# A 256-step recurrence inside a decoder kernel: its weights in four column tiles of 32, its input terms in two of 64 with a filler product behind them

## The reference, cut to what matters

```python
u  = einsum('bsd,nd->bsn', x, Wi) + bi
sp = einsum('bsd,nd->bsn', x, Ws) + bs

def step(state, inp):
    u_t, sp_t = inp
    state = tanh(state @ A.T + u_t @ B.T) + sp_t
    return state, state @ C.T

_, ys = scan(step, zeros, (u, sp))        # 256 steps, one after another
out = einsum('bsn,dn->bsd', ys, Wo) + bo
```

## Time and profile before

| | us |
|---|---|
| median of 3 runs | 1328.63 |
| profiled execution, its own time | 1330.58 |
| span of the profiled execution | 1328.9 |
| PE busy in the span | 1046.6 (79%) |
| ACT busy in the span | 672.7 (51%) |
| DVE busy in the span | 896.4 (67%) |
| recurrence, from the first step's product to step 255's | 1038.89 to 1208.92 |

### The profile page before, as it was taken

One profiled execution on the slowest core, in us unless ns is written; L12 is line 12 of the kernel. 1 busy time (PEld: TensorE's weight loads), 2 busy tenths in 40 slices (PEclk: granted clock), 3 DMA queues, 4 the chain that ended last, 5 costly groups with the idle time before them and its releaser, 6 DMA issues.

```text
span 1328.9 us, 18554 instructions
## 1 busy us (share of the span) xinstructions
PE 1046.6 (79%) x6579; PEld 679.0 (51%) x6579; DVE 896.4 (67%) x2076; ACT 672.7 (51%) x1863; POOL 644.2 (48%) x617
## 2 busy tenths in 40 slices
PE   5667978898788889888888978888854999998321
PEld 3354555465455546545554654555543665664321
DVE  3348776968787796878779687877976000444598
ACT  3746846764684686468468646844520123332000
POOL 1137656746765674676567467656841000111032
PEclk9769998999999999999999999999985679998655
DMA  6000000000000000000000000000000000000301
GB/s 167 1 4 9 1 1 12 1 1 5 8 1 1 13 1 1 5 9 1 1 13 1 1 1 1 1 1 1 1 17 0 0 1 2 7 8 5 32 16 32
DMA packets 56810, 12.76 MB, mean 10 GB/s; under 512 B 40318, under 2 KB 56462, under 8 KB 56590
## 3 DMA queue, kind: packets, MB, share of 16 engines
q1 hardware_dynamic: 56718, 11.58, 4.1%
HBM read 9.46 MB, written 2.12 MB: 9 GB/s over the span
## 4 chain that ended last, share of the span: by engine, by line
PE 40%; DVE 34%; ACT 10%; POOL 10%; issue 4%; DMA 1%; SPq 0%; POOLq 0%; DVEq 0%; ACTq 0%
PE bank_d L1672 5%; PE score_banks L1379 5%; PE score_banks L1731 4%; PE bank_a L1360 4%; DVE qm_s L1025 4%; DVE stats L887 3%; PE score_banks L1381 3%; DVE k_sin L1015 3%; PE score_banks L1380 3%; DVE kr_s L1019 3%; DVE prob L1079 3%; PE score_banks L1402 2%; PE out_bank L1624 2%; DVE o_rec L1071 2%; POOL psum L584 2%
## 5 line engine op out<-in xcount | busy, mean ns | idle before, releaser
L505 POOL TENSOR_TENSOR var_eps<-mv,epsilons 128x2 f32<-128x2 f32 (+2 forms) x64 | 12.7, 199 | 405.9 <-DVE mv L890 405.9
L765 ACT ACTIVATE prob<-score_banks 128x512 f32<-128x512 f32 x256 | 152.5, 596 | 104.3 <-PE score_banks L1381 101.8
L584 POOL TENSOR_TENSOR psum<-psum,prob 128x512 f32<-128x512 f32 x64 | 109.2, 1707 | 121.4 <-DVE prob L1079 120.9
L1379 PE MATMUL score_banks<-qm_s,kr_s 128*128 128x512 f32 x256 | 139.1, 543 | 29.9 <-DVE kr_s L1019 29.0
L1079 DVE TENSOR_SCALAR prob<-prob 128x1024 f32<-128x1024 f32 x128 | 111.1, 868 | 50.0 <-ACT prob L765 49.8
L1559 PE MATMUL out_bank<-prob,v 128*64 128x256 f32 x896 | 115.2, 389 | 2.4 <-DVE on L1072 2.3
L1025 DVE SCALAR_TENSOR_TENSOR qm_s<-q_raw,pair_mask,qm_s 128x256 fp32r<-128x256 f32 x128 | 80.7, 671 | 52.1 <-ACT qm_s L733 52.1
L582 POOL TENSOR_TENSOR psum<-prob 128x512 f32<-128x512 f32 x64 | 92.0, 1437 | 38.3 <-DVE prob L1079 38.3
L1380 PE MATMUL score_banks<-qm_s,kr_s 128*128 128x512 f32 x256 | 108.7, 425 | 0.0
L1381 PE MATMUL score_banks<-qm_s,kr_s 128*128 128x512 f32 x256 | 108.1, 422 | 0.0
L692 ACT ACTIVATE prob<-prob,neg_max 128x128 f32<-128x128 f32 (+1 forms) x256 | 106.2, 421 | 0.0
(11 more groups left out here) (336 smaller groups left out, 2627.0 us busy)
## 6 DMA issues: line engine op xcount, KB each, us to landing
cb<-in_ctx_dram SPq DMA_DIRECT2D x8, 256.0 KB, 2.8
bias_mask<-bias_scratch SPq DMA_DIRECT2D x1, 1536.0 KB, 7.3
xb<-in_x_dram SPq DMA_DIRECT2D x8, 128.0 KB, 2.1
prob<-in_L_xattn_Wkv_dram SPq DMA_DIRECT2D x1, 1024.0 KB, 6.6
att_scratch<-on SPq DMA_DIRECT2D x16, 64.0 KB, 3.1
prob<-att_scratch SPq DMA_DIRECT2D x2, 512.0 KB, 4.0
out_dram<-v SPq DMA_DIRECT2D x4, 256.0 KB, 2.3
prob<-in_L_xattn_Wq_dram SPq DMA_DIRECT2D x1, 512.0 KB, 7.4
```

What stands on the lines that cost most here:

```text
L584: link(g.tensor_tensor(psum[:, p % 2, :], psum[:, p % 2, :], pp[:, 2, :], ALU.add))
L765: s.activation(prob[:, p % 2, kb, :], sc[:, kb % 2, :], ACT.Exp, scale=DH ** -0.5).then_inc(exp_done, 1)
L1379: mm(out_ap, a_high, b_low, start=True, stop=False, **kw)
```

## The change

Three things are edited, all on PE. The product of each step is written in four column tiles of 32 output rows instead of two of 64. Each third of the input terms is written as two products of 64 output rows (columns 0 to 63 and 64 to 127 of the array) instead of one of 128. Behind each of these thirds a filler with 96 columns is added.

```diff
-KEEP = 192
-HALF_ROWS = P // 2
+KEEP, KEEP_Z = 192, 96
+HALF_ROWS, STEP_ROWS = P // 2, P // 4
...
-            def keep_clock():
-
-                mm(bank_d2[0:HALF_ROWS, 0:KEEP], ident[:, 0:HALF_ROWS], w_qkv_t[:, 0:KEEP], start=True, stop=True,
+            def keep_clock(columns=KEEP):
+
+                mm(bank_d2[0:HALF_ROWS, 0:columns], ident[:, 0:HALF_ROWS], w_qkv_t[:, 0:columns], start=True, stop=True,
                    skip_group_check=True)
...
             def z_third(part, third):
 
                 lo = Z_FIRST + P * part
-                bank = cf[:, lo:lo + P]
-                if third == 0:
-                    mm(bank, bwi_t, x3_t[:, lo:lo + P], start=(lo % 512 == 0), stop=False, skip_group_check=True)
...
+                for half in range(0, P, HALF_ROWS):
+                    of = slice(half, half + HALF_ROWS)
+                    bank = cf[of, lo:lo + P]
+                    if third == 0:
+                        mm(bank, bwi_t[:, of], x3_t[:, lo:lo + P], start=(lo % 512 == 0), stop=False,
+                           skip_group_check=True)
...
             def step(t):
                 pe.wait_ge(h_ready, t)
-                for lo in range(0, P, HALF_ROWS):
-                    last = mm(cf[lo:lo + HALF_ROWS, t * B:(t + 1) * B], a_t[:, lo:lo + HALF_ROWS],
+                for lo in range(0, P, STEP_ROWS):
+                    last = mm(cf[lo:lo + STEP_ROWS, t * B:(t + 1) * B], a_t[:, lo:lo + STEP_ROWS],
                               hid[:, (t - 1) * B:t * B], start=False, stop=True, skip_group_check=True)
                 last.then_inc(z_ready, 1)
...
                 if t <= 3 * Z_PARTS:
                     z_third(*divmod(t - 1, 3))
+                    keep_clock(KEEP_Z)
                 else:
                     keep_clock()
```

More of the change, by code:

```diff
@@ L1719, in z_third @@
                 lo = Z_FIRST + P * part
-                bank = cf[:, lo:lo + P]
-                if third == 0:
-                    mm(bank, bwi_t, x3_t[:, lo:lo + P], start=(lo % 512 == 0), stop=False, skip_group_check=True)
[L1723 to L1726, removed]
+                for half in range(0, P, HALF_ROWS):
[4 more added lines that the diff above has]
+                           skip_group_check=True)
+                    elif third == 1:
+                        mm(bank, aws_t[:, of], x3_t[:, lo - B:lo + P - B], start=False, stop=False,
+                           skip_group_check=True)
+                    else:
+                        mm(bank, c_rows[:, D + half:D + half + HALF_ROWS], one_row[:, 0:P], start=False, stop=True,
+                           skip_group_check=True)
             def step(t):
                 pe.wait_ge(h_ready, t)
-                for lo in range(0, P, HALF_ROWS):
-                    last = mm(cf[lo:lo + HALF_ROWS, t * B:(t + 1) * B], a_t[:, lo:lo + HALF_ROWS],
+                for lo in range(0, P, STEP_ROWS):
+                    last = mm(cf[lo:lo + STEP_ROWS, t * B:(t + 1) * B], a_t[:, lo:lo + STEP_ROWS],
                               hid[:, (t - 1) * B:t * B], start=False, stop=True, skip_group_check=True)
```

## The result

The changed kernel takes 1375.61 us (median of 4 runs, 1375.47 to 1377.65) against 1329.03 for the kernel before (4 runs, 1327.88 to 1329.70). The ratio is 1.0355, with a 95% interval from 1.0337 to 1.0373: slower by 3.5%. The forecast was 1332.4 in a range from 1325 to 1352, so it was wrong. It named the mechanism that did this, as a rival with a chance of 0.19, and priced it at 46 us if it struck in the first sixteen late steps, which its range left out.

What follows compares the result with a forecast made beforehand. The recurrence was taken as limited by PE and its drains at tile-shape changes, elsewhere by the chain of product and tanh. -7.8 + 6.0 + 5.6 = +3.8 us gave 1334.4, set to 1332.4 from the runs' median; range 1325 to 1352.

Steps and rivals of the forecast that it cites:

- The step's product in four tiles: Each step's product on PE: ends 0.04 us sooner, 0.25 us after its first load; chain-limited steps take 0.525, not 0.565.
- Filler steps at the full clock: Steps 37 to 127: PE drains at both width changes, 0.655 us a step, 59.6 us against 53.59, 6.0 us lost.
- Steps 1 to 36: Input-term steps: 0.705 us, every third 0.86, at the full clock; 27.2 us against 35.04, a gain of 7.8 us.
- Late steps at the full clock: The 128 late steps: eighty fillers cost 7.2 us, other intervals gain 1.6 us, in sum +5.6 us.
- The clock in the late steps: Rival: clock falls to half there and stays; 6 us if in the last sixteen, 46 in the first; chance 0.19.
- No drain between column tilings: Rival: 32 and 64 rows count as one mode, the chain limits every step, -22.7 us, 1306 us; chance 0.08.
- Tiles one behind the other: Rival: the two input-term tiles run one after the other in steps 1 to 36, +7.7 us, 1340; chance 0.04.
- The clock falling in steps 1 to 36: Rival: clock stays low or falls there, steps 37 to 127 stay at 1.1 us, some 100 us more; chance 0.02.

Runs made afterwards that it cites:

- e2: Changed kernel with step, input terms and fillers of the recurrence all in tiles of 32 rows; 1310.87 us, ratio 0.9857 to the kernel before.
- e1: Changed kernel with its step back in two tiles of 64 rows, the same width as input terms and filler; 1314.08 us, ratio 0.9882 to the kernel before.
- e3: Changed kernel with one filler more behind step 128, the first late step; 1332.20 us, ratio 1.0013 to the kernel before.
- e4: Changed kernel keeping only the four-tile step, input terms back in one product of 128 rows without filler; 1419.12 us, ratio 1.0673 to the kernel before.
- e6: Changed kernel with five fillers of 192 columns ahead of the recurrence, nothing inside it touched; 1431.94 us, ratio 1.0765 to the kernel before.
- e11: Changed kernel with ten fillers ahead of the recurrence; four executions took 1379.18, 1378.31, 1378.92 and 1337.07 us.
- e5: Changed kernel with the recurrence all in 32 rows and the constants' product over 128 input rows, zero-padded; 1307.57 us, ratio 0.9830 to the kernel before.
- e9: Changed kernel with five fillers ahead of the recurrence and the constants' product over 128 input rows; 1376.45 us, ratio 1.0351 to the kernel before.

## Why the prediction was wrong, point by point

*The step's product in four tiles: right on PE, half as large at ACT.* It ends 0.25 us after its first load, as forecast. But tanh starts 0.32 us after that load (1085.26 to 1085.58 in e2), not 0.30: it stands 0.07 us after the product's end, where the earlier trace rows have 0.05. So the gain where the chain limits is 0.02 us a step (0.545 against 0.565), and the forecast had 0.04 (0.525). e2 shows it alone.

*Filler steps at the full clock: right.* 0.648 against 0.655 forecast; +5.3 us against +6.0. The drain from 64 rows to 32, which the forecast took over from the rule and from the way in the other direction, is shown by the changed kernel's rows, and its absence between equal widths by e1 and e2. Where nothing drains a step of 32 rows takes 0.545, so the two drains cost 0.10 us a step.

*Steps 1 to 36: right.* 0.705 and 0.852 against 0.705 and 0.86, at the full clock; -7.9 us against -7.8. The tiles run side by side.

*Late steps at the full clock: right in size,* +5.4 in e3 against +5.6.

*The clock in the late steps: the step that failed.* The forecast summed the late steps as if the clock held, and gave its fall a chance of 0.19. It fell in all 4 executions, in the fifth late step, and the late steps took 129.31 us where the sum had 87.0 (81.40 + 5.6). The working saw the danger in the mean of a sixteen (240 to 270 columns a microsecond) and named as thinnest the stretch "around places 15 to 3". What it missed is that the first sixteen is thinner than the other seven: place 0 has no products there, because `early(b - 1, 16)` starts with the second batch. e3 puts one filler into that hole and 43 us are gone. It also gave the moment at which the hole comes no weight. Its argument against the fall was that the clock had never fallen there before and that the steps of the thin part get shorter. They did not in sum: the step with a filler in the hole got longer by what the others gained, and the hole takes 3.02 us before and after. That it had been harmless before was seen at the moments of the kernel before alone, and was weak ground for setting the fall at 0.19. The price was right: 46 us if in the first sixteen, 42.5 measured ((129.31 - 86.81) us in the late steps). So was the rest of that rival: in a loop with drains the clock doesn't come back (e4, e6).

*The rivals.* No drain between column tilings: refuted by the rows after. Tiles one behind the other: refuted. The clock falling in steps 1 to 36: not in the changed kernel, but in e6, which runs them 1.9 us later. The forecast gave it 0.02 and a price of some 100 us; e6 lies 99.7 us above e3, whose clock holds (1431.94 and 1332.20).

*What stays open.* Whether the kernel before would keep its clock in the hole at the changed kernel's moment; it kept it in every execution on record, but at its own moments. What exactly separates e11's one execution that kept its clock from its other three. And what the chip counts. The runs show that what PE runs in the hole counts (e3) and that a shift of the start counts (e6, e11), and no more. So the fall is shown as the failed step and the hole as its place, while the share that the drains have in it stays open.

## What to carry to other kernels

Count the width of a product's tile as part of its neighbours' cost: here a small product between fillers of another width gained 0.04 us on PE and paid two drains for it (0.648 us a step in place of 0.565), and the fix is to give all of them one width (e2, 1.4% faster than before), input rows too (e5, 1.7%). Where a chain of small products lives by fillers, look for the thinnest place of the order, at the ends of loops and in their first pass above all, not for the mean; a fall there lasts for the whole rest of the chain (42.5 us here), and one filler in the hole costs 0.10 us. A thin place that was harmless in one kernel need not be so after an edit elsewhere: run the kernel at a few shifted starts before trusting it, as e6 and e11 do. A loop that didn't lift the clock once it was down (1.06 us a step, e4 and e6) must be priced at both levels.

## What the runs showed of the hardware that was not expected

Moving an unchanged recurrence by five fillers moved the fall of the clock from its 132nd step to its third (e6), and ten fillers gave both outcomes in one kernel (e11, 1337.07 and 1379.18 us). The early fall came with a product over one input row; with the same columns over 128 rows the clock held (e9), though 0.13 us of the moment differ as well. From trace to trace the changes of the granted clock ahead of the recurrence kept their place relative to the work, within 0.2 us (6.08 to 6.24 us from the last rise to step 1 in the eight kernels without fillers ahead). And the tanh that the profile names beside a weight load (0.28 us of wait for ACT in the filler steps) ended 0.15 us before the load started: the profile has no releaser for a drained array.
